# Four output products in one run behind the key projection

## What is computed

```python
qkv = silu(x @ Wqkv.T)                 # q, k, v for every head
out_nd = einsum(qi * q_decay, kv)      # blocks of 64, kv carries decayed history
qk = einsum(qi, ki) * diag_decay
out = out_nd + einsum(qk, vi)
...
out = out * rms * norm_w
return sigmoid(x @ Wg.T) * out @ Wo.T
```

## Time and profile before

| | |
|---|---|
| median of three executions | 1404.68 us |
| profiled execution | 1402.29 us |
| its span, first to last instruction | 1400.0 us |
| TensorE busy | 1325.2 us, 95% |
| VectorE busy | 1004.2 us, 72% |
| ScalarE busy | 661.1 us, 47% |
| GpSimd busy | 294.7 us, 21% |
| mean granted TensorE clock | 0.982 |
| adds of `YB` to `resid` (line 996) | 256, mean 686 ns |
| a pass of a projection (line 356), as the profile models it | 1024, mean 382 ns |

### The profile page before, as it was taken

How to read it: one execution, slowest core, us unless ns; L and a number is a source line. 1 busy time by engine, 2 the same in 40 slices (tenths; PEclk the granted TensorE clock), 3 DMA queues, 4 the chain that set the end, 5 groups by cost and what they waited for, 6 DMA issues and landing times.

```text
span 1400.0 us, 21497 instructions
## 1 busy us (share of the span) xinstructions
PE 1325.2 (95%) x6940; PEld 785.1 (56%) x6940; DVE 1004.2 (72%) x1862; ACT 661.1 (47%) x1198; POOL 294.7 (21%) x212
## 2 busy tenths in 40 slices
PE   5999999998999999999999999999995769999997
PEld 2556656665566566656656666665653435555553
DVE  6776776766676867677776767666679567888763
ACT  3634344342434343434434343434353458888754
POOL 2201111010101010111101010101027444555540
PEclk9999999999999999999999999999997889999999
DMA  5001121111101010101111010000000010111000
GB/s 203 1 24 60 38 79 53 47 60 38 45 23 45 25 58 22 45 22 45 39 36 45 22 45 7 30 7 30 23 31 30 16 45 17 44 45 46 31 16 30
DMA packets 14437, 55.03 MB, mean 39 GB/s; under 512 B 2112, under 2 KB 2112, under 8 KB 12096
## 3 DMA queue, kind: packets, MB, share of 16 engines
q1 hardware_dynamic: 14400, 54.55, 11.2%
HBM read 50.35 MB, written 4.19 MB: 39 GB/s over the span
## 4 chain that ended last, share of the span: by engine, by line
PE 76%; DVE 11%; issue 5%; ACT 4%; POOL 2%; DVEq 0%; DMA 0%; POOLq 0%; ACTq 0%; SPq 0%
PE bank L356 15%; PE bank L357 14%; PE bank L358 14%; PE bank L425 4%; PE bank L427 4%; PE bank L426 4%; PE bank L534 3%; PE bank L535 3%; PE bank L407 2%; PE bank L391 2%; PE bank L415 1%; DVE w_hi L948 1%; PE bank L404 1%; DVE bb L1207 1%; POOL den L1481 1%
## 5 line engine op out<-in xcount | busy, mean ns | idle before, releaser
L356 PE MATMUL bank<-x_hi,w_hi 128*128 128x512 f16 x1024 | 391.0, 382 | 7.9 <-DVE w_lo L951 5.5
L357 PE MATMUL bank<-x_lo,w_hi 128*128 128x512 f16 x1024 | 389.6, 381 | 0.0
L358 PE MATMUL bank<-x_hi,w_lo 128*128 128x512 f16 x1024 | 389.4, 380 | 0.0
L1426 POOL TENSOR_TENSOR sq_sum<-sq_sum,o_sq 128x512 f32<-128x512 f32 x64 | 103.4, 1615 | 832.9 <-ACT o_sq L676 832.9
L996 DVE TENSOR_TENSOR resid<-resid,bank 128x512 f32<-128x512 f32 x256 | 173.2, 686 | 83.7 <-PE bank L427 82.0
L356 PEld LDWEIGHTS bank<-x_hi,w_hi 128*128 128x128 f16 x1024 | 100.8, 98 | 136.1 <-issue 41.4
L358 PEld LDWEIGHTS bank<-x_hi,w_lo 128*128 128x128 f16 x1024 | 100.5, 98 | 121.6 <-issue 1.7
L357 PEld LDWEIGHTS bank<-x_lo,w_hi 128*128 128x128 f16 x1024 | 100.8, 98 | 93.1 <-issue 1.4
L1002 DVE SCALAR_TENSOR_TENSOR gated<-g_t,bank 128x512 f32<-128x512 f32 x64 | 44.0, 687 | 131.2 <-PE bank L407 131.2
L425 PE MATMUL bank<-wo_hi,u_hi 128*128 128x512 f32 x256 | 125.5, 490 | 2.9 <-DVE resid L996 1.4
L671 ACT ACTIVATE v_t<-bank,dq 128x512 f32<-128x512 f32 x64 | 44.0, 687 | 175.7 <-PE bank L358 175.7
(11 more groups left out here) (160 smaller groups left out, 2531.1 us busy)
## 6 DMA issues: line engine op xcount, KB each, us to landing
w_raw<-w_ffn SPq DMA_DIRECT2D x32, 512.0 KB, 3.3
raw<-w_heads SPq DMA_DIRECT2D x15, 1024.0 KB, 4.8
raw<-w_heads SPq DMA_DIRECT2D x17, 256.0 KB, 2.8
x_in<-x_rows SPq DMA_DIRECT2D x8, 512.0 KB, 3.9
val<-ctx_t SPq DMA_DIRECT2D x8, 512.0 KB, 3.2
out<-y_out SPq DMA_DIRECT2D x8, 512.0 KB, 2.6
resid<-x_t SPq DMA_DIRECT2D x3, 1024.0 KB, 8.4
resid<-x_t SPq DMA_DIRECT2D x4, 256.0 KB, 4.0
```

The costliest lines, as they stand in the source:

```text
L356: mm(PJ[j % 2][:, :], a, c, start=kt == 0, stop=False)
L357: mm(PJ[j % 2][:, :], a, d, start=False, stop=False)
L358: last = mm(PJ[j % 2][:, :], b, c, start=False, stop=kt == KT - 1)
L1426: g_.tensor_tensor(sq_sum[:, g, :], sq_sum[:, g, :], o_sq[:, :], ALU.add).then_inc(sq_added, 1)
```

## The change

On TensorE the first two `output` calls leave their place between Q and K, and all four stand between K and V. On VectorE the four adds leave their two places and stand together behind `split_k`. Nothing else is touched: the same instructions, the same banks, the same waits.

```diff
@@ TensorE, unit
-                if lag2:
-                    output(before2, u - 2, 0)
-                    output(before2, u - 2, 1)
                 project(h, g, K)
                 if lag2:
-                    output(before2, u - 2, 2)
-                    output(before2, u - 2, 3)
+                    for tt in range(4):
+                        output(before2, u - 2, tt)
                 project(h, g, V)
@@ VectorE, unit
-                if lag2:
-                    add_y(u - 2, (g - 2) % GROUPS, 0)
-                    add_y(u - 2, (g - 2) % GROUPS, 1)
                 if lag1:
                     split_probs(u - 1)
                 split_q(u)
...
+                split_k(u)
                 if lag2:
-                    add_y(u - 2, (g - 2) % GROUPS, 2)
-                    add_y(u - 2, (g - 2) % GROUPS, 3)
-                split_k(u)
+                    for tt in range(4):
+                        add_y(u - 2, (g - 2) % GROUPS, tt)
```

## The result

| | before | after |
|---|---|---|
| median | 1404.47 us (4 runs) | 1493.78 us (4 runs, 1493.11 to 1496.17) |
| ratio | | 1.0641, 95% interval 1.0623 to 1.0660 |
| span of the profiled execution | 1400.0 us | 1490.7 us |

The kernel became 6.4% slower: 89.3 us between the medians, 90.7 between the spans. The forecast was 1489 in a range of 1470 to 1512.

The account below looks back on a forecast made before the run. TensorE was taken to bound the attention. Ordinary units 51.8, table-load units 26.0, head 0 3.0 and last unit 3.9 made 84.7 us, so 1487.0 profiled; plus 2.4 to the median, 1489 us, range 1470 to 1512.

Parts of the forecast that it names:

- The sum: All units with output products: together 84.7 us added to the profiled execution of 1402.29 us, giving 1487.0.
- What bounds: Attention: TensorE sets the time, so gaps opened inside units add to the end; 3.4 us of weight waits stay.
- An ordinary unit: 45 units, heads 1 to 15: product 2 waits 1.05 us for add 0, restart 0.10; price 1.15 us each.
- Units with g = 2: Heads 1 to 14, 14 units: table load delays `p_hi` and so `k_t`; price 1.86 us each.
- That product 3 does not wait: Each unit's run of four: add 1 releases at 5.89 us, before product 3 would start at 6.04.
- Head 0: Its two units with output products: priced 1.15 + 1.86 = 3.0 us, up to 2 more.
- The last unit: Head 15: adds behind next-stage work, TensorE waits some 7.8 us, what follows is 3.9 us late; bounds 0 and 7.3.
- The clock: Rival: TensorE's clock falls at each unit's wait, costing 2 us more per unit, 1609 us in all; chance 4%.
- No change: Rival: in the run of four, adds keep pace with products through two alternating banks, 1405 us; chance 3%.
- Faster: Rival: one weight-load seam per unit goes, 0.27 us in 62 units, 16.7 us saved, 1388 us; chance 3%.

Follow-up runs that it names:

- the kernels with additions: Changed kernel plus two or four small unused VectorE additions between the split of K and the adds, heads 1 to 14: 1538.99 us and 1651.18 us.
- the experiment: Changed kernel with the last unit of head 15 back in its old order on both engines: 1489.31 us.
- The kernel with four banks where they fit: Changed kernel with products 2 and 3 in two other PSUM banks; head 0 and last two units of head 15 in the old order: 1403.25 us.
- with four banks: Changed kernel, products 2 and 3 in `VT` and `OT`; last unit in old order, g = 2 unit of head 15 on two banks: 1406.15 us.

## Why the prediction held, step by step

- **The sum**: 84.7 us were forecast for the profiled execution and 90.7 measured. The 6.0 that were missing are 1.45 ahead of the first output product, 0.7 in head 0, 2.4 in heads 1 to 14 and 1.5 behind the start of the last unit. The forecast of the median is off by only 4.8: I had kept 2.4 between the profiled execution and the median, and it was 0.7. That part of the closeness is luck.
- **What bounds**: TensorE sets the time. Of the 1.07 to 1.76 us that it waits in each unit of heads 1 to 14 nothing came back: the waits for weights stayed at 3.3 us, as forecast.
- **An ordinary unit** (K's last matmul at 2.60, `k_t` 3.01, `k_hi` 3.73, `k_lo` 4.18, add 0 4.52, product 2 at 5.25, each from Q's last matmul): measured 2.59, 3.00, 3.73, 4.18, 4.52 and 5.25. The price of 1.15 is what the units show. The eight units that follow ternary work lost 0.10 more; I had left that out.
- **Units with g = 2**: 1.86, measured 1.83 to 1.87, and the cause, a `p_hi` that is late behind the table load, was shown by moving `p_hi`; that it acts by `k_t` alone was not.
- **That product 3 does not wait**: so in the timeline, and there is but one wait in each unit.
- **Head 0**: 3.7 against 3.0, inside the 2 us allowed, but not as I had priced it. The wait was 3.49 and not 1.76, and 1.05 of waiting for `xmax` went. The clock stayed at 1.00 behind it; in the kernels with additions it fell behind the same wait.
- **The last unit**: the mechanism was right and its size off. The term "TensorE waits some 7.8 us, what follows is 3.9 late" measured 9.0 and 5.4 (3.8 to 4.5 by the experiment, which is close to my 3.9). What made the wait longer is the split of K itself: I took 1.37 from the earlier trace rows, and it took 2.55, with a multiplication of 2.52 on GpSimd beside it. The scores came at 1147.06 - 85.3 = 1061.8, where I had 1061.5, and the masks 4.4 late; the rest arose further on.
- **The clock**: I gave its fall 4%, on the ground that waits of 2.58 and 1.43 had left it at 1.00. For the changed kernel that came out right. As an argument it was weak: waits of 2.28 brought it down in 52 of 61 units, and the one of 3.49 in head 0 left it up here but brought it down in the two kernels with additions. One case at full clock is no evidence for sixty.
- **What I had no term for, ahead of the first output product**: 1.45 us, where both kernels run the same instructions on TensorE. 0.83 of it is there when the first projection begins (12.83 us against 12.00); behind that 12 matmuls start 0.43 apart and not 9. The kernel with four banks where they fit has head 0 in the order of before and shows 1.43 too, and other kernels show from -0.08 to 1.63. So it is no effect of the changed order.
- **What I had no term for, the first unit of head 5**: 1.5 more than the others. TensorE has just waited 3.9 and 1.2 us for the thresholds in both kernels and is slow afterwards in both (granted clock 0.73 over 340 to 346 us before, 0.68 over 366.5 to 376 after). The slow stretch of work is longer after: 5.7 us from the end of the wait, where it was 2.9. Half of the difference is 1.4, so the clock accounts for nearly all of the 1.5. Why it stays down longer is open; the same unit grows by 1.08 with the adds in their old place and by 0.24 with four banks.
- **"No change", because the eviction keeps pace**: the rule of the Trainium skill ("Perfetto Trace Analysis", section on matmuls), that groups which rotate through banks hide the eviction, held in a run of four for four banks and not for two: with two and the adder standing by, 0.35 a unit was left.
- **"Faster", by the seam that goes**: the seam is worth about 0.02 a unit in the run with four banks where it fits, and not the 0.27 that the idle time of the weight loads suggests.

## What to carry to other kernels

When products that rotate through n banks are put in a run, work out when the reader of the first bank can start, by following that reader's queue back through whatever stands ahead of it, other engines included; product n+1 waits for that, however short the eviction is. A place between two batches of other work is cover for a slow reader, and moving the products away gives it up; with enough banks the same order is free. And a wait has two prices: its own length, and, if it is long, sometimes that of the clock.

## What was unexpected in the hardware

For a wait that comes back in every unit, the behaviour of TensorE's clock turned between a cost of 1.86 us and one of 2.5: of the 98 units at 1.86 or below in the changed kernel and the one with two additions none lost more than the wait and 0.10, but for the first of head 5, and 94 of the 117 units at 2.5 to 2.56 lost 1.65 us more, the granted clock at half for a stretch behind the wait. Length was not all: two waits of the same 2.28 us, 20 us apart, went one way each, and so did the wait of 3.49 or 3.50 us in head 0 in two kernels. And the profile's wait is shorter than what TensorE loses, by 0.15 to 0.25 us, since it begins at the modelled end of a matmul: with the adds in their old place a loss of 0.35 us a unit, 21 us in 60 units, left no line among the waits.
